# Float16 parts for the first attention's output product and the feed-forward's products

## The reference

```python
x = x + attn_a(_layernorm(x))   # 16 heads of 64
x = x + ffn(_layernorm(x))
x = x + attn_b(_layernorm(x))   # 8 heads of 128, rotated, causal
x = x + ffn(_layernorm(x))
# attn_a: w = softmax(scores); attn = w @ V, (2048, 1024)
y = x + (attn @ Wo.T + bo)
return layernorm(y) * gamma + beta
# ffn
h = relu(x @ W1 + b1)           # 128 -> 512
return h @ W2 + b2              # 512 -> 128
```

## Time and profile before

| what | value |
|---|---|
| median of three executions | 1936.58 us (1933.06 to 1937.72) |
| the profiled execution | 1935.38 us, span 1933.6 us |
| busy PE | 1865.8 us, 96% of the span |
| busy DVE, ACT, POOL | 1420.6, 1546.5 and 1598.4 us |
| instructions | 55434 |
| traffic to and from HBM | 9.20 MB, 5 GB/s |

### The profile page before, as it was taken

One profiled execution on the slowest core, in us unless ns is written; L12 is line 12 of the kernel. 1 busy time (PEld: TensorE's weight loads), 2 busy tenths in 40 slices (PEclk: granted clock), 3 DMA queues, 4 the chain that ended last, 5 costly groups with the idle time before them and its releaser, 6 DMA issues.

```text
span 1933.6 us, 55434 instructions
## 1 busy us (share of the span) xinstructions
PE 1865.8 (96%) x23343; PEld 1267.0 (66%) x23343; DVE 1420.6 (73%) x2613; ACT 1546.5 (80%) x1919; POOL 1598.4 (83%) x1025
## 2 busy tenths in 40 slices
PE   4899999999999999999999999779999999999998
PEld 3566666666666666666666666547777777767766
DVE  7788778778777878877877875566767767767652
ACT  4799999999998898898898899646666666666664
POOL 3899999999999999999999999358787787887752
PEclk8999999999999999999999999889999999999999
DMA  6101101100100100100100100100000000000000
GB/s 147 35 11 26 34 14 23 35 15 21 35 18 19 34 19 18 35 18 18 35 18 18 35 2 2 55 1 2 2 1 2 2 2 1 2 1 2 2 2 23
DMA packets 45032, 37.94 MB, mean 20 GB/s; under 512 B 8304, under 2 KB 44144, under 8 KB 44528
## 3 DMA queue, kind: packets, MB, share of 16 engines
q1 hardware_dynamic: 44304, 34.00, 7.5%
q10 hardware_dynamic: 480, 0.39, 0.1%
HBM read 8.15 MB, written 1.05 MB: 5 GB/s over the span
## 4 chain that ended last, share of the span: by engine, by line
PE 81%; POOL 8%; issue 5%; DVE 4%; ACT 1%; DMA 0%; ACTq 0%; POOLq 0%; DVEq 0%
PE ST L1594 11%; PE ST L1595 11%; PE RING L1479 7%; PE OO L1560 6%; PE OO L1562 6%; POOL PBUF L695 6%; PE OO L1559 6%; PE OO L1479 4%; PE ST L1787 2%; PE ST L1794 2%; PE ST L1793 2%; PE ST L1792 2%; PE ST L1659 2%; PE OO L1680 1%; PE RING L1572 1%
## 5 line engine op out<-in xcount | busy, mean ns | idle before, releaser
L611 POOL TENSOR_TENSOR PAB<-PR,PAB 128x1024 f16<-128x1024 f32 x342 | 724.1, 2132 | 48.3 <-ACT PAB L787 47.6
L787 ACT ACTIVATE PAB<-ST,exp_scale 128x1024 f16<-128x1024 f32 x512 | 567.5, 1108 | 0.0
L1089 DVE TENSOR_REDUCE maxes<-RING 128x1 f32<-128x512 f32 x661 | 440.3, 685 | 132.1 <-PE RING L1479 127.7
L1559 PE MATMUL OO<-VP,PAB 128*128 128x66 f16 x4096 | 446.7, 192 | 2.4 <-POOL PAB L611 2.4
L1560 PE MATMUL OO<-VP,PAB 128*128 128x64 f16 x4096 | 447.2, 193 | 0.0
L1562 PE MATMUL OO<-VP,PAB 128*128 128x66 f16 x4096 | 445.2, 192 | 0.0
L785 ACT ACTIVATE PR<-ST,exp_scale 128x1024 f32<-128x1024 f32 x342 | 381.7, 1116 | 73.4 <-PE ST L1595 70.7
L1559 PEld LDWEIGHTS OO<-VP,PAB 128*128 128x128 f16 x4096 | 380.5, 96 | 77.3 <-issue 15.4
L1560 PEld LDWEIGHTS OO<-VP,PAB 128*128 128x128 f16 x4096 | 377.1, 97 | 61.3
L1594 PE MATMUL ST<-QL,KH 128*128 128x512 f16 x1024 | 388.6, 379 | 1.9 <-DVE QH L1101 1.0
L1595 PE MATMUL ST<-QH,KL 128*128 128x512 f16 x1024 | 388.8, 380 | 0.0
(11 more groups left out here) (305 smaller groups left out, 3962.0 us busy)
## 6 DMA issues: line engine op xcount, KB each, us to landing
KH<-HS SPq DMA_DIRECT2D x124, 64.0 KB, 2.0
QL<-HS SPq DMA_DIRECT2D x64, 64.0 KB, 2.0
QL<-LS SPq DMA_DIRECT2D x64, 64.0 KB, 2.1
QH<-HS SPq DMA_DIRECT2D x64, 64.0 KB, 2.0
KL<-LS SPq DMA_DIRECT2D x62, 64.0 KB, 2.0
X<-in_L_attn_a_x SPq DMA_DIRECT2D x4, 256.0 KB, 3.8
SHARED<-in_rope_cos SPq DMA_DIRECT2D x1, 1024.0 KB, 4.9
SHARED<-in_rope_sin SPq DMA_DIRECT2D x1, 1024.0 KB, 7.0
```

Of the source, the lines that this page charges most:

```text
L611: pool.tensor_tensor(PB[:, s, :], PRA[g % PR_SLOTS], PA[:, s, :], ALU.subtract).then_inc(p_low_ready, 1)
L787: act.activation(PA[:, step % SLOTS_A, :], ST[step % 2][:, :], ACT.Exp, scale=scale).then_inc(sa.exps, 1)
L1089: dve.reduce_max(maxes[:, i // BLOCKS, i % BLOCKS:i % BLOCKS + 1], bank[:, :], X_AXIS).then_inc(sa.ring_taken, 1)
L1559: pe.matmul(o, high, v[:, 0:V2_AT], start=(m == 0 and qt == 0), stop=False, skip_group_check=True)
```

## The change

The weights `Wo`, `W1` (with `b1`) and `W2` get float16 pairs. Their squares are taken by ACT ahead of the first attention, summed by DVE in unit 2 (`sum_squares_wo`, `sum_squares_fw`) and put through the same powers of two as the second attention's weights (columns `OUT_A`, `FW1`, `FW2`). The pairs of `Wo` are made in unit 4 of the first iteration (high on ACT, low in `split_wo` on DVE), those of `W2` in unit 5, where DVE also scales `W1` and `b1` in place (`scale_fw`); `W1`'s pair is made in the second attention (`split_w1`).

The output product then runs from `ATH` and `ATL`, 12 float16 products instead of 4 float32 ones, and `take_output_a` multiplies by the inverse scale while it adds. The second product of both feed-forwards has 48 float16 products instead of 32 float32 records. For this the relu writes float32 to `HIDF`, DVE casts it to float16 (`high_hidden`), and POOL subtracts (`low_hidden`). `HIDF` has one buffer in each round, so that a relu waits for the subtraction of the block before. The first product of the first feed-forward stays float32; that of the last has three float16 products, for which the settled rows are split to `XH` and `XL` (`take_settled`, `last_block`, `low_block`).

```diff
@@ POOL
-            for b in range(BLOCKS):
-                add_b2(0, b)
+            def low_hidden(r, b):
+                for j in range(CH):
+                    n = (r * BLOCKS + b) * CH + j
+                    pool.wait_ge(hid_high, n + 1)
+                    pool.tensor_tensor(HID[b % 2][:, 1, j, :], HIDF[:, j, :], HID[b % 2][:, 0, j, :], ALU.subtract
+                                       ).then_inc(hid_low, 1)
+            add_b2(0, 0)
+            add_b2(0, 1)
+            low_hidden(0, 0)
+            add_b2(0, 2)
+            low_hidden(0, 1)
...
@@ ACT
+            act.activation(wo_squares[:, :], WoT.rearrange("p j c -> p (j c)"), ACT.Square,
+                           scale=float(np.sqrt(D))).then_inc(b_squared, 1)
...
+                if (u, step) == (5, 3):
+                    act.wait_ge(b_scaled, 1)
+                    act.activation(W2H[:, :, :], W2s[:, :, :], ACT.Copy, scale=b_up[:, FW2:FW2 + 1]).then_inc(fw_high, 1)
+                if (u, step) == (4, 4):
+                    act.wait_ge(b_scaled, 1)
+                    act.activation(WOH[:, :, :], WoT, ACT.Copy, scale=b_up[:, OUT_A:OUT_A + 1]).then_inc(wo_high, 1)
...
-                wait(act, ffn_put, r * BLOCKS + b - 1)
-                act.activation(HID[b % 2][:, j, :], QUARTER[j], ACT.Relu, bias=b1c[:, j:j + 1]
-                               ).then_inc(hid_ready, 1)
+                wait(act, hid_low, n - CH + 1)
+                act.activation(HIDF[:, j, :], QUARTER[j], ACT.Relu, bias=b1c[:, j:j + 1]).then_inc(hid_full, 1)
@@ DVE
             def take_turned(s, bank, item):
                 dve.wait_ge(s.ring_put, item + 1)
-                dve.tensor_copy(AT[:, :], bank[:, :]).then_inc(s.ring_taken, 1)
+                link(dve.tensor_copy(ATH[:, :], bank[:, :]))
+                dve.tensor_tensor(ATL[:, :], bank[:, :], ATH[:, :], ALU.subtract).then_inc(s.ring_taken, 1)
...
+                dve.tensor_tensor(fw_back[:, :], b_down[:, FW1:FW1 + 1], b_down[:, FW2:FW2 + 1], ALU.mult)
+                dve.tensor_scalar(W1B1[:, :], W1B1[:, :], b_up[:, FW1:FW1 + 1], None, ALU.mult).then_inc(fw_scaled, 1)
...
+                dve.scalar_tensor_tensor(W2L[:, :, :], W2s[:, :, :], b_up[:, FW2:FW2 + 1], W2H[:, :, :], ALU.mult,
+                                         ALU.subtract).then_inc(fw_low, 1)
...
+                dve.scalar_tensor_tensor(WOL[:, :, :], WoT, b_up[:, OUT_A:OUT_A + 1], WOH[:, :, :], ALU.mult,
+                                         ALU.subtract).then_inc(wo_low, 1)
...
+            def take_output_a(bank, item, qb):
+                dve.wait_ge(sa.ring_put, item + 1)
+                a = XN[:, qb * BT:(qb + 1) * BT, :].rearrange("p a c -> p (a c)")
+                dve.scalar_tensor_tensor(a, bank[:, :], b_down[:, OUT_A:OUT_A + 1], a, ALU.mult, ALU.add
+                                         ).then_inc(sa.ring_taken, 1)
...
+            def high_hidden(r, b, j):
+                n = (r * BLOCKS + b) * CH + j
+                dve.wait_ge(hid_full, n + 1)
+                wait(dve, ffn_put, r * BLOCKS + b - 1)
+                dve.tensor_copy(HID[b % 2][:, 0, j, :], HIDF[:, j, :]).then_inc(hid_high, 1)
...
-                dve.tensor_tensor(a, a, O[1][:, :].rearrange("p (a c) -> p a c", c=D), ALU.add
-                                  ).then_inc(x_ready, 1)
+                dve.scalar_tensor_tensor(a, O[1][:, :], fw_back[:, 0:1], a, ALU.mult, ALU.add).then_inc(x_ready, 1)
@@ PE, output_a
+                high, low = WOH[:, pair, :], WOL[:, pair, :]
                 for i in range(BT):
-                    ins = pe.matmul(RING3[item % 3][:, i * D:(i + 1) * D], AT[:, i * P:(i + 1) * P], WoT[:, pair, :],
-                                    start=True, stop=True)
+                    o, q = RING3[item % 3][:, i * D:(i + 1) * D], slice(i * P, (i + 1) * P)
+                    pe.matmul(o, ATH[:, q], high, start=True, stop=False)
+                    pe.matmul(o, ATH[:, q], low, start=False, stop=False)
+                    ins = pe.matmul(o, ATL[:, q], high, start=False, stop=True)
@@ PE, hidden_part
+                if r == 0:
+                    pe.matmul(QUARTER[j], W1s[:, part], XNT[:, q], start=True, stop=True).then_inc(hid_put, 1)
+                else:
+                    pe.matmul(QUARTER[j], W1H[:, part], XH[:, q], start=True, stop=False)
...
@@ PE, ffn_out
+                        high, low = (HID[b % 2][:, a, j, i * P:(i + 1) * P] for a in range(2))
+                        pe.matmul(o, high, W2H[:, j, :], start=(j == 0), stop=False)
+                        pe.matmul(o, high, W2L[:, j, :], start=False, stop=False)
+                        ins = pe.matmul(o, low, W2H[:, j, :], start=False, stop=(j == CH - 1))
@@ PE, the end
+            turn_block(3 * BLOCKS + 2, 2, TURN_LAST[0])
             ffn_out(1, 0)
-            for b in range(2, BLOCKS):
-                pe.wait_ge(xn_ready, 3 * BLOCKS + b + 1)
-                wait(pe, xnt_ready, 3 * BLOCKS + b - 2)
-                turn_block(3 * BLOCKS + b, b, O[0])
-                hidden(1, b)
-                ffn_out(1, b - 1)
+            pe.wait_ge(xn_ready, 3 * BLOCKS + 4)
+            turn_block(3 * BLOCKS + 3, 3, TURN_LAST[1])
+            hidden(1, 2)
+            ffn_out(1, 1)
+            hidden(1, 3)
+            ffn_out(1, 2)
             ffn_out(1, 3)
```

More of the change, by code:

```diff
@@ L93 @@
 LIFT_B = float(np.log(2.0 ** 4))
+OUT_A = 3 * HB
+FW1 = 3 * HB + 1
+FW2 = 3 * HB + 2
+SCALES_B = 3 * HB + 3
 def steps_b(qb):
@@ L705, in _ @@
                     low_b((head + 1) % 2, j, (head + 1) * 2 * BLOCKS + j, F[:, j % 2, :])
-            for b in range(BLOCKS):
-                add_b2(1, b)
+            add_b2(1, 0)
+            add_b2(1, 1)
+            low_hidden(1, 0)
+            add_b2(1, 2)
+            low_hidden(1, 1)
+            add_b2(1, 3)
+            low_hidden(1, 2)
+            low_hidden(1, 3)
         @block.scalar
@@ L902, in _ @@
                         values_high_b(1 - hs, item[1], RING3B[n % 3], n)
+                if (it, ul, step) == (0, 6, 1):
+                    act.wait_ge(fw_scaled, 1)
+                    act.activation(W1H[:, :], W1s, ACT.Copy).then_inc(fw_high, 1)
                 if head + 2 < HB and (qb, step) == (2, 10):
@@ L1202, in _ @@
                     normalise_a((u - 1) % UNITS_A, u)
+                if u == 2 and step in (2, 4):
+                    sum_squares_fw(step // 2 - 1)
                 if u == 2 and step in (5, 6, 7):
                     sum_squares_b(step - 5)
+                if (u, step) == (5, 1):
+                    scale_fw()
+                if (u, step) == (5, 6):
+                    split_w2()
+                if (u, step) == (2, 3):
+                    sum_squares_wo()
                 if u == 3 and step >= 4:
                     scale_heads_b(step - 4)
+                if (u, step) == (4, 1):
+                    scale_heads_b(4)
+                if (u, step) == (4, 6):
+                    split_wo()
                 for n, item in ITEMS_A[g]:
@@ L1254, in _ @@
             scale_and_shift(BLOCKS + 6)
+            def high_hidden(r, b, j):
[3 more added lines that the diff above has]
+                dve.tensor_copy(HID[b % 2][:, 0, j, :], HIDF[:, j, :]).then_inc(hid_high, 1)
+            for j in range(CH):
+                high_hidden(0, 0, j)
             settle(7)
             scale_and_shift(BLOCKS + 7)
+            for j in range(CH):
+                high_hidden(0, 1, j)
             def take_ffn(r, b):
@@ L1323, in _ @@
             settle_ffn(0)
+            for j in range(CH):
+                high_hidden(0, 2, j)
             settle_ffn(1)
+            for j in range(CH):
+                high_hidden(0, 3, j)
             low_block(BLOCKS + 1, 0, TURN_B[0])
@@ L1361, in _ @@
                 place = g - (len(PLACES_B) - TILES)
+                if (it, ul, step) == (0, 6, 4):
+                    split_w1()
                 if place == 1:
@@ L1398, in _ @@
             take_output(sbb, RING3B[(n + 1) % 3], n + 1, X, BLOCKS - 1)
+            for j in range(2):
+                high_hidden(1, 0, j)
             dve.wait_ge(sbb.ring_taken, n + 2)
             last_ln(3)
+            for j in range(2, CH):
+                high_hidden(1, 0, j)
             normalise(4 * BLOCKS + 3, 3)
-            for b in range(BLOCKS):
+            for j in range(CH):
+                high_hidden(1, 1, j)
+            low_block(2 * BLOCKS + 1, 2, TURN_LAST[0])
+            take_ffn(1, 0)
+            low_block(2 * BLOCKS + 2, 3, TURN_LAST[1])
+            for j in range(CH):
+                high_hidden(1, 2, j)
+            take_ffn(1, 1)
+            for j in range(CH):
+                high_hidden(1, 3, j)
+            for b in range(2, BLOCKS):
                 take_ffn(1, b)
@@ L1490, in total_b @@
                 claim_a(item)
-                pe.wait_ge(b_summed, 3)
-                pe.matmul(RING3[item % 3][:, 0:3 * HB], ones_f[:, :], b_sums[:, :], start=True, stop=True
+                pe.wait_ge(b_summed, 6)
```

(2 more changed lines are left out.)

106 lines of the change are left out of this document (78 added, 28 removed).

## The result

The median of 20 executions is 1939.32 us (1937.03 to 1943.72), against 1936.18 us (1932.08 to 1938.47) for 20 of the kernel before. The ratio is 1.0023, with a 95% interval from 1.0016 to 1.0030: 3 us slower, inside the 0.3% that was called no change, and 0.3 us from the predicted 1939.0. The profiled execution, with 1937.03 us one of the two fastest of the 20, has a span of 1935.2 us, 1.6 more than before.

A forecast was written before the change was run, and what follows sets the result against it. PE bounds the first attention; between the attentions and at the end a DVE, ACT, POOL chain does. -9.3 + 3 + 0.5 + 6.4 + 2.0 = +2.6, giving 1939.2, rounded 1939 us: no change; range 1926 to 1948.

The forecast's parts named there:

- The saving: First attention's output product: 0.67 instead of 0.97 us per item on PE, 31 items, 9.3 us saved.
- The rival that it isn't realised: Output product: float16 products cost 0.97 us in the loop, or DVE's longer item stops PE; +9 to +12, 1950, chance 0.05.
- Preparation: Inside the first attention: some 9.8 us of added DVE time reaches PE as +3 us (ends 0 and +9.8).
- The ratio: First attention's preparation: similar work with 5.8 us more DVE time made PE wait 1.4, so 9.8 gives 2.4.
- The pair: Feed-forwards: a DVE cast and the POOL subtraction that follows cost 0.33 + 1.12 = 1.45 us together.
- the lockout: Feed-forwards: DVE's cast and POOL's subtraction shut each other out completely; the rival without it gave 1922, chance 0.20.
- the cast's price: DVE's 128x512 cast goes at half price per column: 0.42 us long, 0.33 from one to the next.
- First feed-forward: Between the attentions: the longer chain of casts and subtractions costs +6.4 us; first projection at 1267.4 instead of 1261.01.
- Last feed-forward: Last stage: PE's list shrinks by 8 us, but pairs of cast and subtraction set the time, +2.0 us.
- Sixteen pairs: Last feed-forward: sixteen pairs of cast and subtraction at 1.45 us, 23.2 us, with the bias additions among them.
- my third rival: Both feed-forwards: gaps in PE's work drop its clock, two or three products at half speed; about +8, 1947, chance 0.09.
- The second attention: Second attention: making W1's pair (split_w1) and a wait for it cost +0.5 us.

The follow-up runs named there:

- e10: The change with each cast of the hidden rows made twice, nothing left out: 1948.17 us, 8.8 more than the change.
- e6: The change with DVE's addition and statistics of the last settled block moved ahead of block 0's casts in the first feed-forward: 1936.36 us, 3.0 less than the change.
- e1: The change with the second product of both feed-forwards back in float32, all preparation kept: 1929.99 us, ratio 0.9964 to the kernel before.
- e4: The change with DVE's cast replaced by a second relu on ACT into float16, POOL still subtracting: 1928.38 us, 11 less than the change.
- e9: e5 with POOL's four short weight-scaling operations moved behind the first multiplication by gamma: 1922.65 us, 1.8 less than e5.
- e5: e1 with everything that prepares W2 taken out: 1924.48 us, 5.5 less than e1.
- e7: The change with 10 and 9 unused products filling PE's last two waits before the last feed-forward products: 1937.41 us, 1.9 less than the change.

## Why the prediction was right

**The saving** (-9.3): right in size, 0.67 us an item and 0.29 saved; DVE's longer item never stopped PE, since the rest of the attention shortened by just these items in all runs with it. The rival that it isn't realised is refuted. The Trainium skill's 81 ns per pair of load and product ("TensorE: Matmul & The Clock Gate", "Back-to-back issue gap") doesn't hold here either: 56 ns.

**Preparation** (+3): start and iteration 0 together are 3.3 us longer, with 0.9 saved there, so 4.2 in this profile, and 3.1 to 6.6 over the other runs with the same preparation, so 1.2 over the forecast is less than this stretch differs by itself. Of the 4.2, 2.9 are waits of PE on DVE's reductions (5.2 us instead of 2.3, from 50 to 205 us). The ratio gave 2.4: its size was nearly right, its picture wrong. I had given each instruction half a POOL operation to wait; the two at unit 5 waited for a whole one each, one behind the other, and cost PE 3.1 us in one piece.

**The pair** (1.45): the lockout was right, and so was the cast's price, 0.41 us. The step that failed is the sum 0.33 + 1.12: the pair took 1.28, so the two overlap by 0.17. e10 shows that one more cast costs its whole 0.33 nevertheless.

**First feed-forward** (+6.4, first projection 7.6 later): 8.0 later in the profile. By the prediction's count, eleven pairs at 1.28 gave back 1.9 us of it; the hold of 3.1 us at the end of the attention, of which the prediction knew nothing, took 2.2. The count itself is not borne out (e10 cost 6.2 us here, not 3.6), so the 1.9 is an estimate. The order of the steps was right (e6).

**Last feed-forward** (+2.0): +1.3. Sixteen pairs, a count that e10 confirms, at 1.28 instead of 1.45 are 2.7 less, and the half clock in the last product 1.6 more. That was my third rival, of which I had thought that it would come in two or three products or in none; it came in one.

**The second attention** (+0.5) came out 2.7 us shorter, for two reasons. I had foreseen that PE catches up 1.2 us behind the first projection; by the projection that stood at 1261.01 before it had caught up 1.0. Most of the rest, 1.7 us, has to do with the change only by accident and is the clock: a stretch at its lower level that the trace of before has near 1877 is missing in the change. The same stretch of both kernels, before first:

```profile
1877.00:1880.50 3.50, 3.50 (x21) 2.42 (x20) 0.75 (x1) 1.02 (x2) 2.11 (x2) 0.51 0.00 0
```
```profile
1877.00:1880.50 3.50, 2.64 (x23) 1.67 (x24) 0.71 (x3) 3.04 (x6) 2.66 (x3) 1.00 0.00 0
```

So the total was met to 0.3 us by errors that cancel: +1.2 for the preparation, +2.2 for the hold and +1.6 for the clock at the end, against -1.9 and -2.7 for the pairs and -2.0 in the second attention. That leaves +1.0 of the +2.6, nearer the 1.6 us between the two traces than the 3.1 between the medians; single executions of either kernel differ by more than that. That the number came so close is luck: the hold and the two stretches of clock were in no term of the sum. What the experiments do bear out is the mechanism (a saving on PE spent on DVE's and POOL's pairs) in e1, e4 and e10.

## What to carry to other kernels

Splitting an operand into float16 parts paid where the product was on a saturated PE and the split on an engine with time to spare (0.29 us an item), and cost 9 us where PE waited for the split: price the chain of the split first. Let the two halves of a split run on engines that don't hold each other up (here ACT and POOL, not DVE and POOL), but not both on one engine that has other work in the chain. And keep tiny two-input instructions away from a busy POOL's queue: one column cost 2.1 us.

## What I had not expected of the hardware

A held DVE instruction doesn't always get in when POOL's running operation ends: 3.10 us through four further operations in the change, 0.90 in the kernel before, by nothing that the profile shows but the moment. What decides it stays open; e9 only moved POOL's operations.

Cast and subtraction exclude each other but for 0.17 us of 1.45. And a stretch of half clock (3.4 us) near the end of the second attention came and went without a change of its instructions: before, e1, e5, e7 and e9 have it and took 641.4 to 641.6 us for the second attention, the others don't and took 637.4 to 639.1.
